# A fused adaLN transformer block on one core: two issuing queues for the second group's stacked rows, and the decay table loaded and exponentiated earlier

## The chip, the cores and the metric

The kernel runs on one core of a Trainium2 chip. That core has a matrix engine (TensorE, PE in the profile), VectorE (DVE), ScalarE (ACT), GpSimd (POOL) and a queue engine that only issues transfers (SyncE, SP). ScalarE can issue transfers too, between its own instructions. The engines run side by side and wait for each other through semaphores written out by hand. The metric is the device time of one execution in microseconds (us); shorter is better.

## The reference

```python
x = L0_attn_x                                       # (8, 256, 128)
mod = (_silu(L0_c) @ L0_wmod).reshape(8, 6, 1, -1)
sa, ca, ga, sb, cb, gb = (mod[:, k] for k in range(6))
ga = (2 * (ga >= 0) - 1) * jnp.maximum(jnp.abs(ga), 0.25)      # gb likewise
h = _layernorm(x) * (1 + ca) + sa
x = x + ga * attention(h)                           # 16 heads of 8
h = _layernorm(x) * (1 + cb) + sb
x = x + gb * moe(h)                                 # 16 experts, top 2, plus a shared one
# attention:
scores = einsum('bqhd,bkhd->bhqk', q, k) * 8 ** -0.5
decay = jnp.exp(-alpha * |i - j|)
attn = softmax(scores * decay);  out = (attn @ v) @ Wo.T + bo
```

All values are float32. Eight sequences of 256 tokens are computed.

## The kernel before, in words

The 2048 tokens are cut into four chunks of 512 (two sequences each). In each chunk the attention runs in eight "quads" q = 0 to 7: a quad is four heads of one sequence, and two quads (one per sequence) make a group g of heads. For one quad PE computes four score matrices (`scores`, L914), DVE multiplies them by the decay table and takes the row maximum (`head`, L681), POOL turns them into maximum minus score (`negdiff`, L279), PE transposes them (`turn`, L930, in two halves of two heads), ACT takes the exponential (`exps`, L384) and PE multiplies by the values (`values`, L942). PE's program interleaves them: scores of quad q, first half of the turn of quad q-1, values of quad q-2, second half of the turn of quad q-1. After the four chunks comes the mixture of experts (from L1148 on PE).

The scores need float32 accuracy from faster matmuls. So q and k are split in a high and a low part (`qk_hi_of` on ACT, L362, and `qk_lo_of` on DVE, L601), and for each head the four combinations high/high, high/low, low/high and low/low are stacked as rows of one 32-row operand. The stacking is done by transfers: `stack_slot` (L148) copies 32 partitions of q and k, 128 KB, into every fourth partition of `qk_st`, and a group needs its four slots before its scores can start. Slot 0 needs the two high parts, slot 2 the low part of q, slots 1 and 3 the low part of k. Group 0 of chunk 0 is made in another way (`first`, `first_hi`, `first_lo`), without transfers. All other groups are stacked by SP (`stack`, L181), in the order group 1, 2, 3 of chunk 0 and then the later chunks. For group 1 SP issues slot 0, 2, 1, 3, one after the other.

The prologue, before that: SP loads the first half of chunk 0 of x, the conditioning, its weights, an identity, the other half of x, the first weights, then the table of lags (`load(decay...)`, L176), and more. ACT issues three small loads (L503 to L505), computes the SiLU of the conditioning and one dummy exponential that brings in the table of functions. DVE computes the layer norm of the first two tiles (`stats_first`, `xn_first`), then copies the modulation vectors, then waits for lags and alpha and negates alpha (L789 to L790). PE fills its waits with matmuls on zeros (`warm`, L1100), transposes the normalised tiles (`lnt_first`), and ACT makes the first affine copy (`h_first(0)`, L523), then the exponential of the lags (L526), then `first_hi(0)`. In chunk 0 POOL computes the layer norm constants of chunk 1 (`ln1(1)`) before the maximum differences of head 8, ACT then normalises chunk 1's tiles (`xn_of(1)`, L357), and PE transposes them (`lnt(1)`) right after the scores of quad 3 and ahead of the turn of quad 2.

Of the kernel before, what the change touches and what calls it, by code (L numbers as in the profile page):

```python
# [10 lines left out]
ALU = mybir.AluOpType  # L11
ACT = mybir.ActivationFunctionType
AX_X = mybir.AxisListType.X

P = 128
# [12 lines left out]
SLOTS = 4  # L28
# [22 lines left out]
def build(nc, x, x_t, c_t, w_first, v_first, w_attn, vecs, alpha, w_r, w_gu, w_d, w_mod, lag, ident, out):  # L51
# [3 lines left out]
    with ExitStack() as ctx:  # L55
        def sb(name, shape, dt=F32):
            return ctx.enter_context(nc.sbuf_tensor(name, shape, dt))
# [6 lines left out]
        decay = sb("decay", [P, BPC, SEQ])  # L64
        alpha_sb, nalpha = sb("alpha_sb", [P, 1]), sb("nalpha", [P, 1])
# [82 lines left out]
        def stack_slot(eng, g, slot):  # L148
            bq, bk = SLOT_BLOCKS[slot]
            eng.dma_start(qk_st[slot:P:SLOTS, :, g, :].bitcast(F32),  # L150
                          qk[32 * g:32 * g + 32, bq:bk + 1:bk - bq, :].bitcast(F32)).then_inc(s_st[g], 16)
# [13 lines left out]
        @block.sync  # L165
        def _(sp):
            def load(ap, dram, done):
                sp.dma_start(ap, dram).then_inc(s[done], 16)  # L168

            load(x_all[:, 0:BPC, :], x_v[:, 0:BPC, :], "ld_x0")  # L170
            load(ct_sb[:], c_t, "ld_ct")
            load(wmod_sb[:, SA:CA1 + 1, :], w_mod[:, SA:CA1 + 1, :], "ld_mod")
            load(id_f[:], ident, "ld_id")
            load(x_all[:, BPC:TT, :], x_v[:, BPC:TT, :], "ld_x0b")
            load(wf_sb[:], w_first, "ld_first")
            load(decay[:], lag, "ld_decay")  # L176
            load(wmod_sb[:, GA_IN:, :], w_mod[:, GA_IN:, :], "ld_mod_b")
            load(wa_sb[:], w_attn, "ld_attn")
            load(x_all[:, TT:, :], x_v[:, TT:, :], "ld_x")

            def stack(c, g):  # L181
                if c:
                    if g == 0:
                        sp.wait_ge(s["qk_lo_ok"], c * 2 + 2)
                    sp.wait_ge(s["s_done"], (c - 1) * STEPS + 8 * g + 8)
                    for slot in range(SLOTS):
                        stack_slot(sp, g, slot)
                    return
                for slot, (done, count) in ((0, ("qk_hi_ok", 2)), (2, ("qk_lo_ok", 1)),
                                            (1, ("qk_lo_ok", 2)), (3, ("qk_lo_ok", 2))):  # L190
                    if g == 1:
                        sp.wait_ge(s[done], count)
                    stack_slot(sp, g, slot)

            def weights_out(c):
                sp.wait_ge(s["cwt_ok"], c + 1)
                sp.dma_start(cw_dram[c], cw_t[:]).then_inc(s["cw_out"], 16)

            def weights_in(c, u):
                if c:  # L200
                    sp.wait_ge(s["mul_done"], (c - 1) * ROUTED + u + 1)
                for k in range(2):
                    e = 2 * u + k
                    sp.dma_start(cwb[k * FE:k * FE + FE, u, :],
                                 cw_dram[c, e:e + 1, :].to_broadcast([FE, CHUNK])).then_inc(s_cwb[u], 16)

            def out_of(c):
                cols = slice(c * CHUNK, c * CHUNK + CHUNK)
                sp.dma_start(out[:, cols], xt[:, cols]).then_inc(s_out, 16)

            for c in range(NCHUNK):
                for g in range(NG):
                    if c or g:
                        stack(c, g)
                    if c == 0 and g == NG - 1:
                        for ap, dram in ((wr_sb[:], w_r), (wgu_sb[:], w_gu), (wd_sb[:], w_d)):
                            load(ap, dram, "ld_ffn")
                for k in {1: (0,), 2: (1,), NCHUNK - 1: (2, 3)}.get(c, ()):
                    sp.wait_ge(s["wlo_ok"], 2 * k + 2)
                    cols = slice(k * CHUNK, k * CHUNK + CHUNK)  # L220
                    sp.dma_start(xt[:, cols], x_t[:, cols]).then_inc(s_xt[k], 16)
            weights_out(0)
            sp.wait_ge(s["cw_out"], 16)
            for u in range(ROUTED):
                weights_in(0, u)
            weights_out(1)

            for c in range(NCHUNK):
                for u in range(ROUTED):
                    if c + 1 < NCHUNK:  # L230
                        if u == 0:
                            sp.wait_ge(s["cw_out"], 16 * (c + 2))
                        weights_in(c + 1, u)
                    if u == LAG_D + 2 and c:
                        sp.wait_ge(s["y_added"], c)
                        out_of(c - 1)
                if c + 2 < NCHUNK:
                    weights_out(c + 2)
            for b in range(BPC):
                cols = slice((NB - BPC + b) * SEQ, (NB - BPC + b + 1) * SEQ)  # L240
                sp.wait_ge(s["y_added"], NCHUNK + b)
                sp.dma_start(out[:, cols], xt[:, cols]).then_inc(s_out, 16)
            sp.wait_ge(s_out, 16 * (NCHUNK + 1))
# [98 lines left out]
        def _(act_e):  # L342
# [19 lines left out]
            def qk_hi_of(c, i, ps):  # L362
                act_e.wait_ge(s["qk_mm"], c * 2 + i + 1)
                if c and i == 0:
                    act_e.wait_ge(s_st[NG - 1], c * STACK)
                nc.scalar.activation(qk[:, (Q_HI, K_HI)[i], :], ps[:], ACT.Identity,
                                     bias=vec_sb[:, (B_Q, B_K)[i]:(B_Q, B_K)[i] + 1],
                                     scale=1.0).then_inc(s["qk_hi_ok"], 1)
# [108 lines left out]
            def chunk(i):  # L477
                prev, nxt = i > 0, i < NCHUNK - 1
                for q in range(QUADS):
# [20 lines left out]
                    if (i, q) in SPLITS:  # L500
                        split(SPLITS.index((i, q)))

            act_e.dma_start(vf_sb[:], v_first).then_inc(s["ld_vf"], 16)  # L503
            act_e.dma_start(alpha_sb[:], alpha.to_broadcast([P, 1])).then_inc(s["ld_decay"], 16)
            act_e.dma_start(vec_sb[:], vecs).then_inc(s["ld_attn"], 16)  # L505
            act_e.wait_ge(s["ld_ct"], 16)
            nc.scalar.activation(silu_c[:], ct_sb[:], ACT.Silu).then_inc(s["silu_ok"], 1)
            act_e.wait_ge(s["pool_init"], 1)
            nc.scalar.activation(spare[:], nhalf[:], ACT.Exp)

            def h_first(b, ready, done):
                act_e.wait_ge(s[ready], 1)
# [8 lines left out]

            act_e.wait_ge(s["modt_ok"], 2)
            h_first(0, "lnt_a", "h_a")  # L523
            act_e.wait_ge(s["ld_decay"], 32)
            act_e.wait_ge(s["nalpha_ok"], 1)
            nc.scalar.activation(decay[:], decay[:], ACT.Exp, scale=nalpha[:, 0:1]).then_inc(s["decay_raw"], 1)  # L526
            act_e.wait_ge(s["ld_vf"], 16)
            first_hi(0)
            h_first(1, "lnt_done", "h_ok")
            first_hi(1)  # L530
            qk_hi_of(0, 0, ps_t[0])
            qk_hi_of(0, 1, ps_t[1])
            for i in range(NCHUNK):
                chunk(i)
            exps(NCHUNK - 1, QUADS - 1, 0)
# [53 lines left out]
        def _(dve):  # L589
# [171 lines left out]
            def stats_first(tiles_, loaded, st_done, done):  # L761
                dve.wait_ge(s[loaded], 16)
                for t in tiles_:
                    last = nc.vector.bn_stats(stats[:, t, :], x_all[:, t, :])
                last.then_inc(s[st_done], 1)
                dve.wait_ge(s[st_done], 1)
                for t in tiles_:
                    last = nc.vector.bn_aggr(mv[:, t, :], stats[:, t, :])
                last.then_inc(s[done], 1)

            def xn_first(tiles_, ready, done):
                dve.wait_ge(s[ready], 1)
                for t in tiles_:
                    last = nc.vector.tensor_scalar(xn[:, t, :], x_all[:, t, :], mv[:, t, 0:1], rstd[:, t:t + 1],
                                                   ALU.subtract, ALU.mult)
                last.then_inc(s[done], 1)
# [5 lines left out]
                                               ALU.subtract).then_inc(s["first_ok"], 1)  # L782

            stats_first(range(0, BPC), "ld_x0", "stats_a", "mv_a")
            xn_first(range(0, BPC), "rstd_a", "xn_a")
            dve.wait_ge(s["modt_mm"], 1)
            nc.vector.tensor_copy(mod_t[:, SA, :], ps_s[0][:, 0:NB]).then_inc(s["modt_ok"], 1)
            nc.vector.tensor_scalar(mod_t[:, CA1, :], ps_s[0][:, NB:2 * NB], 1.0, None, ALU.add).then_inc(s["modt_ok"], 1)
            dve.wait_ge(s["ld_decay"], 32)  # L789
            nc.vector.tensor_scalar(nalpha[:], alpha_sb[:], -1.0, None, ALU.mult).then_inc(s["nalpha_ok"], 1)  # L790
            stats_first(range(BPC, TT), "ld_x0b", "stats_ok", "mv_ok")
            first_lo(0, 0)
            first_lo(0, 1)
# [92 lines left out]
        def _(pe):  # L886
# [213 lines left out]
            def warm(n, ps=ps_o):  # L1100
                for k in range(n):
                    mm(ps[:, 0:P], attn_t[:, 0:P], attn_t[:, 0:P])
# [15 lines left out]
            def first(b, k):  # L1118
                mm(ps_first[2 * b + k][:, 0:SEQ], wf_sb[:, k, :], h_t[:, seq_cols(b)]).then_inc(s["first_mm"], 1)

            warm(2)
            pe.wait_ge(s["ld_id"], 16)
            lnt_first(0, "xn_a", "lnt_a")
            warm(3)
# [141 lines left out]
```

## Time and profile before

| | us |
|---|---|
| median of 3 runs (lowest, highest) | 242.24 (242.0, 243.11) |
| the profiled execution, its own time | 243.98 |
| the span of that profile | 242.2 |
| PE / DVE / ACT / POOL busy | 230.0 / 192.3 / 161.8 / 188.8 |

Times in the rows below count from the start of the span. The span is 1.8 us shorter than that execution's own time, and the execution was 1.7 us longer than the median run. "Idle before" is the time for which an engine stood still ahead of an instruction, with what ended it. An engine name with a q (SPq, ACTq) is its sequencer, and a DMA_DIRECT2D on it is the issue of one transfer.

### The profile page before, as it was taken

How to read it: one execution, taken by the hardware profiler on the slowest of the kernel's cores; microseconds unless marked ns; L12 is line 12 of the kernel's file. 1: busy time of each engine (PE TensorE's matmuls, PEld its weight loads, DVE VectorE, ACT ScalarE, POOL GpSimd, SP SyncE). 2: the span in 40 equal slices, each digit the busy share in tenths (PEclk: the TensorE clock that was granted, in tenths of full speed). 3: DMA queues.
4: the chain of work that ended last, by engine and by line, in shares of the span. 5: the costliest groups of instructions: out<-in, count | busy, mean ns of one | idle time of the engine just before them, and what ended most of it. 6: DMA issues, size and time to landing. Idle time of an engine off the chain costs nothing.

```text
span 242.2 us, 5876 instructions
## 1 busy us (share of the span) xinstructions
PE 230.0 (95%) x1866; PEld 171.5 (71%) x1866; DVE 192.3 (79%) x800; ACT 161.8 (67%) x318; POOL 188.8 (78%) x343
## 2 busy tenths in 40 slices
PE   7996999998999999999999999999999999999994
PEld 7764666766657767657767766677888888788882
DVE  3697868898799799899989997469656786985763
ACT  4455668667866798866896578576647758565550
POOL 5579778899999999997999999718477554676661
PEclk9998899999999999999999999999999999999998
DMA  5718902760004730004755500014223340036311
GB/s 131 228 25 193 305 38 54 186 155 3 0 4 102 201 91 4 0 3 117 187 144 186 164 0 5 3 47 131 102 78 131 126 136 1 0 91 198 110 43 43
DMA packets 15342, 22.81 MB, mean 94 GB/s; under 512 B 3088, under 2 KB 5776, under 8 KB 15184
## 3 DMA queue, kind: packets, MB, share of 16 engines
q1 hardware_dynamic: 14880, 22.44, 32.7%
q8 instruction: 15, 0.25, 0.4%
q14 instruction: 15, 0.12, 0.2%
q10 hardware_dynamic: 432, 0.01, 0.1%
HBM read 13.39 MB, written 1.18 MB: 60 GB/s over the span
## 4 chain that ended last, share of the span: by engine, by line
PE 60%; POOL 14%; DVE 12%; ACT 5%; DMA 3%; issue 2%; SPq 2%; DVEq 0%; ACTq 0%
PE bank L888 60%; POOL sc L285 12%; DVE sc L686 4%; DVE sc L852 2%; DMA decay<-in_lag 1%; DMA qk_st<-qk 1%; SPq L168 1%; ACT L553 1%; SPq L150 1%; DVE h_lo L634 1%; DVE pr L846 1%; DVE qk L604 1%; POOL rstd L258 1%; DVE qk_st L780 1%; ACT act_hi L544 1%
## 5 line engine op out<-in xcount | busy, mean ns | idle before, releaser
L285 POOL TENSOR_SCALAR sc<-sc,mx 128x256 f32<-128x256 f32 x256 | 122.2, 496 | 7.8 <-DVE mx L686 7.7
L686 DVE CUSTOM_DVE_ANT_0 sc<-bank,decay 128x256 f32<-128x256 f32 x256 | 91.4, 420 | 14.6 <-PE bank L888 14.3
L389 ACT ACTIVATE pr<-bank 128x512 f32<-128x512 f32 x128 | 69.6, 597 | 25.3 <-PE bank L888 25.1
L888 PE MATMUL bank<-id_f,sc 128*128 128x128 f32 x512 | 69.5, 278 | 2.2 <-ACT pr L389 1.1
L332 POOL TENSOR_TENSOR act_lo<-sc,act_hi 128x512 fp32r<-128x512 f32 x35 | 45.3, 1296 | 33.2 <-ACT act_hi L544 33.2
L888 PEld LDWEIGHTS bank<-id_f,sc 128*128 128x128 f32 x512 | 56.8, 142 | 14.9 <-issue 6.7
L888 PE MATMUL bank<-pr,v_one 128*32 128x256 f32 x512 | 35.1, 393 | 0.0
L846 DVE TENSOR_TENSOR pr<-bank,cwb 128x512 f32<-128x512 f32 x32 | 22.0, 688 | 14.5 <-PE bank L888 14.2
L553 ACT ACTIVATE bank<-bank 128x512 f32<-128x512 f32 x32 | 18.6, 582 | 18.7 <-PE bank L888 18.4
L852 DVE TENSOR_TENSOR sc<-pr,bank 128x512 f32<-128x512 f32 x36 | 24.7, 687 | 5.8 <-ACT bank L553 2.7
L888 PE MATMUL bank<-h_hi,wgu_hi 128*128 128x512 f32 x72 | 28.5, 395 | 0.0
L888 PE MATMUL bank<-h_lo,wgu_hi 128*128 128x512 f32 x72 | 28.1, 391 | 0.0
L888 PE MATMUL bank<-h_hi,wgu_lo 128*128 128x512 f32 x72 | 28.0, 389 | 0.0
L544 ACT ACTIVATE act_hi<-sc 128x512 fp32r<-128x512 f32 x36 | 22.5, 624 | 3.7 <-DVE sc L852 3.4
L888 PEld LDWEIGHTS bank<-pr,v_one 128*32 128x32 f32 x512 | 13.5, 110 | 13.3 <-issue 5.0
L686 DVE DVE_READ_ACCUMULATOR2_ANT mx<- 128x1 f32 x256 | 21.2, 83 | 0.0
L888 PE MATMUL bank<-qk_st 32*128 32x256 f32 x256 | 16.3, 327 | 4.4 <-DMA qk_st<-qk 2.0
L888 PEld LDWEIGHTS bank<-qk_st 32*128 32x128 f32 x256 | 9.8, 183 | 10.0 <-issue 6.1
L888 PEld LDWEIGHTS bank<-h_hi,wgu_hi 128*128 128x128 f32 x72 | 13.5, 188 | 3.1 <-issue 0.4
L888 PEld LDWEIGHTS bank<-h_lo,wgu_hi 128*128 128x128 f32 x72 | 13.5, 188 | 2.9
L888 PEld LDWEIGHTS bank<-h_hi,wgu_lo 128*128 128x128 f32 x72 | 13.5, 188 | 2.7
L888 PE MATMUL bank<-act_hi,wd_hi 128*128 128x512 f32 x36 | 15.0, 416 | 0.0
(105 smaller groups left out, 281.6 us busy)
## 6 DMA issues: line engine op xcount, KB each, us to landing
cwb<-cw_dram SPq DMA_DIRECT2D x64, 128.0 KB, 3.0
qk_st<-qk SPq DMA_DIRECT2D x60, 128.0 KB, 2.7
wgu_sb<-in_w_gu SPq DMA_DIRECT2D x1, 1152.0 KB, 5.7
wgu_sb<-in_x_t SPq DMA_DIRECT2D x4, 256.0 KB, 3.9
x_all<-in_x SPq DMA_DIRECT2D x1, 768.0 KB, 6.5
out_dram<-wgu_sb SPq DMA_DIRECT2D x3, 256.0 KB, 3.1
wd_sb<-in_w_d SPq DMA_DIRECT2D x1, 576.0 KB, 6.6
x_all<-in_x SPq DMA_DIRECT2D x2, 128.0 KB, 2.6
```

The costliest lines, as they stand in the source:

```text
L150: eng.dma_start(qk_st[slot:P:SLOTS, :, g, :].bitcast(F32), qk[32 * g:32 * g + 32, bq:bk + 1:bk - bq, :].bitcast(F32)).then_inc(s_st[g], 16)
L168: sp.dma_start(ap, dram).then_inc(s[done], 16)
L258: nc.gpsimd.tensor_tensor(rstd_[:], var_[:], nhalf[:], ALU.pow).then_inc(s[done], 1)
L285: last = nc.gpsimd.tensor_scalar(sc[:, n % RING, t, :], sc[:, n % RING, t, :], -1.0, mx[:, n % RING, t:t + 1], ALU.mult, ALU.add)
L332: nc.gpsimd.tensor_tensor(act_lo[:, (i * NU + u) % FR, :], act[:, (i * NU + u) % FR, :], act_hi[:, (i * NU + u) % FR, :].bitcast(F32), ALU ...
L389: nc.scalar.activation(pr[:, n % RING, :, :].rearrange("p a b -> p (a b)"), turn_bank(i, n)[:], ACT.Exp, scale=-1.0).then_inc(s["exp_done" ...
L544: nc.scalar.activation(act_hi[:, (i * NU + u) % FR, :], act[:, (i * NU + u) % FR, :], ACT.Copy).then_inc(s["ahi_ok"], 1)
L553: nc.scalar.activation(gate[:], gate[:], ACT.Silu).then_inc(s["silu_done"], 1)
L686: last = nc.vector.tensor_tensor_reduce(sc[:, n % RING, t, :], ps_s[n % SB][:, t * SEQ:t * SEQ + SEQ], decay[:, t, :], float(HD) ** -0.5, ...
L846: nc.vector.tensor_tensor(gate_u[:, n % 2, :], up[:], cwb[:, u, :], ALU.mult).then_inc(s["mul_done"], 1)
L852: nc.vector.tensor_tensor(act[:, r, :], gate_u[:, n % 2, :], (gate if u < ROUTED else up)[:], ALU.mult).then_inc(s["act_ok"], 1)
L888: return nc.tensor.matmul(o, l, r, start=start, stop=stop, skip_group_check=not check, is_transpose=transpose or None)
```

## The change

The second group's (g = 1) four stacking transfers in chunk 0 are shared between two queues: SP issues slots 2 and 1, ACT issues slots 0 and 3. Alpha and the lags are issued by ACT as its first two loads, instead of SP's seventh and ACT's second. The exponential of the lags stands ahead of `h_first(0)` on ACT, and the negation of alpha with its wait for both loads stands ahead of `xn_first` on DVE. PE's filler ahead of the first transposes is one matmul instead of two.

```diff
@@ sync
             load(wf_sb[:], w_first, "ld_first")
-            load(decay[:], lag, "ld_decay")
             load(wmod_sb[:, GA_IN:, :], w_mod[:, GA_IN:, :], "ld_mod_b")
...
-                for slot, (done, count) in ((0, ("qk_hi_ok", 2)), (2, ("qk_lo_ok", 1)),
-                                            (1, ("qk_lo_ok", 2)), (3, ("qk_lo_ok", 2))):
-                    if g == 1:
-                        sp.wait_ge(s[done], count)
+                if g == 1:
+                    sp.wait_ge(s["qk_hi_ok"], 2)
+                    sp.wait_ge(s["qk_lo_ok"], 1)
+                    stack_slot(sp, g, 2)
+                    sp.wait_ge(s["qk_lo_ok"], 2)
+                    stack_slot(sp, g, 1)
+                    return
+                for slot in range(SLOTS):
                     stack_slot(sp, g, slot)
@@ scalar
+            act_e.dma_start(alpha_sb[:], alpha.to_broadcast([P, 1])).then_inc(s["ld_decay"], 16)
+            act_e.dma_start(decay[:], lag).then_inc(s["ld_decay"], 16)
             act_e.dma_start(vf_sb[:], v_first).then_inc(s["ld_vf"], 16)
-            act_e.dma_start(alpha_sb[:], alpha.to_broadcast([P, 1])).then_inc(s["ld_decay"], 16)
             act_e.dma_start(vec_sb[:], vecs).then_inc(s["ld_attn"], 16)
...
             nc.scalar.activation(spare[:], nhalf[:], ACT.Exp)
+            act_e.wait_ge(s["ld_decay"], 32)
+            act_e.wait_ge(s["nalpha_ok"], 1)
+            nc.scalar.activation(decay[:], decay[:], ACT.Exp, scale=nalpha[:, 0:1]).then_inc(s["decay_raw"], 1)
...
             h_first(0, "lnt_a", "h_a")
-            act_e.wait_ge(s["ld_decay"], 32)
-            act_e.wait_ge(s["nalpha_ok"], 1)
-            nc.scalar.activation(decay[:], decay[:], ACT.Exp, scale=nalpha[:, 0:1]).then_inc(s["decay_raw"], 1)
             act_e.wait_ge(s["ld_vf"], 16)
...
             qk_hi_of(0, 1, ps_t[1])
+            act_e.wait_ge(s["qk_hi_ok"], 2)
+            stack_slot(act_e, 1, 0)
+            act_e.wait_ge(s["qk_lo_ok"], 2)
+            stack_slot(act_e, 1, 3)
@@ vector
             stats_first(range(0, BPC), "ld_x0", "stats_a", "mv_a")
+            dve.wait_ge(s["ld_decay"], 32)
+            nc.vector.tensor_scalar(nalpha[:], alpha_sb[:], -1.0, None, ALU.mult).then_inc(s["nalpha_ok"], 1)
             xn_first(range(0, BPC), "rstd_a", "xn_a")
...
-            dve.wait_ge(s["ld_decay"], 32)
-            nc.vector.tensor_scalar(nalpha[:], alpha_sb[:], -1.0, None, ALU.mult).then_inc(s["nalpha_ok"], 1)
@@ tensor
-            warm(2)
+            warm(1)
```

## Rows read from the trace of the kernel before

**Rows 1.** Page, the costliest group: count, busy us, mean ns, idle before, releaser.
```profile
L285 POOL TENSOR_SCALAR sc<-sc,mx 128x256 f32<-128x256 f32 x256 | 122.2, 496 | 7.8 <-DVE mx L686 7.7
```
**Rows 2.** Chain of waits: start us, us, what; first stretch to 40 us.
```profile
3.67 3.51 DMA decay<-in_lag
...
14.23 1.41 DVE qk L604 x2
...
15.67 1.80 SPq L150
...
17.51 0.61 SPq L150
...
18.17 3.01 DMA qk_st<-qk
```
**Rows 3.** Timeline of PE: start us, us, operation, idle before and its releaser.
```profile
5.50 0.69 PE L888 MATMUL bank<-attn_t 128*128 128x128 f32 x4
...
18.07 1.12 PE L888 MATMUL bank<-id_f,sc 128*128 128x128 f32 x8 [0.34 <-POOL sc L285]
21.22 0.51 PE L888 MATMUL bank<-qk_st 32*128 32x256 f32 x8 [2.03 <-DMA qk_st<-qk]
21.66 1.37 PE L888 MATMUL bank<-id_f,sc 128*128 128x128 f32 x8
22.95 1.94 PE L888 MATMUL bank<-pr,v_one 128*32 128x256 f32 x16
...
26.27 0.51 PE L888 MATMUL bank<-qk_st 32*128 32x256 f32 x8
26.71 0.66 PE L888 MATMUL bank<-id_f,xn 128*128 128x128 f32 x4
27.20 1.04 PE L888 MATMUL bank<-id_f,sc 128*128 128x128 f32 x8
28.17 1.07 PE L888 MATMUL bank<-pr,v_one 128*32 128x256 f32 x16
```
**Rows 4.** Stretches: us, busy of PE, PEld, DVE, ACT, POOL, clock, DMA share, GB/s.
```profile
20.00:22.00 2.00, 0.78 (x11) 0.65 (x12) 0.55 (x5) 0.00 (x0) 1.83 (x5) 1.00 0.85 205
22.50:25.50 3.00, 3.00 (x22) 1.40 (x21) 2.93 (x17) 2.58 (x6) 2.98 (x8) 0.50 0.85 189
```
**Rows 5.** Timeline of POOL and of ACT around the second group.
```profile
22.52 0.20 POOL L263 TENSOR_TENSOR nmr<-nmean,rstd 128x4 f32<-128x4 f32 x1
...
27.69 3.70 POOL L285 TENSOR_SCALAR sc<-sc,mx 128x256 f32<-128x256 f32 x8 [1.27 <-DVE mx L686]
32.51 0.94 POOL L285 TENSOR_SCALAR sc<-sc,mx 128x256 f32<-128x256 f32 x2 [1.12 <-DVE mx L686]
...
17.33 1.09 ACT L389 ACTIVATE pr<-bank 128x512 f32<-128x512 f32 x2 [2.49 <-PE bank L888]
23.56 1.64 ACT L357 ACTIVATE xn<-x_all,nmr,rstd 128x128 f32<-128x128 f32 x4
```
**Rows 6.** The DMA queues while SP issues slot 2 (15.7 to 17.4 us).
```profile
q8 instruction: 1, 0.02, 4.6%
...
qk_st<-qk SPq DMA_DIRECT2D x1, 128.0 KB, 3.9
```
**Rows 7.** Timeline of ACT and DVE in the prologue.
```profile
4.17 0.21 ACT L507 ACTIVATE silu_c<-ct_sb 128x8 f32<-128x8 f32 x1 [0.76 <-DMA ct_sb<-in_c_t]
5.70 0.21 ACT L509 ACTIVATE spare<-nhalf 128x4 f32<-128x4 f32 x1
6.52 0.56 ACT L344 ACTIVATE h_t<-bank,mod_t 128x256 f32<-128x256 f32 x1 [0.61 <-PE bank L888]
7.46 0.72 ACT L526 ACTIVATE decay<-decay,nalpha 128x512 f32<-128x512 f32 x1 [0.38 <-DVE nalpha L790]
8.09 1.00 ACT L519 ACTIVATE act_hi<-bank,vf_sb 128x256 fp32r<-128x256 f32 x2
4.97 0.60 DVE L774 TENSOR_SCALAR xn<-x_all,mv,rstd 128x128 f32<-128x128 f32 x2 [1.11 <-POOL rstd L311]
```
## The prediction

> **What bounds the kernel now.** I read three views in this order. The page first: PE is busy for 230.0 of 242.2 us, and the costliest group on another engine is POOL's maximum differences, 122.2 us of work with 7.8 us of idle time before it, 7.7 of that spent waiting for DVE's maxima [rows 1]. So PE sets the pace of the attention and POOL runs close behind it. What the change can give back must therefore be a place where PE stands still, and it must pass POOL as well. The chain of waits next: up to 21 us it leaves PE twice for a transfer, once for the lags, 3.51 us from their issue, and once for the four slots of group 1 [rows 2]. There the reader sees DVE finish the low parts at 15.64, the issue of slot 2 take 1.80 us where that of slot 1 takes 0.61, and the last slot land 3.01 us after its issue began, at 21.18 [rows 2]. PE's timeline last: PE ends the second half-turn of quad 0 at 18.07 + 1.12 = 19.19, stands still for 2.03 us, and starts the scores of quad 2 at 21.22 [rows 3]. After that stop its clock is granted at 0.50 from 22.5 to 25.5, which is the lower of its two levels, 1.2 GHz, where it had 1.00 between 20 and 22 [rows 4]. The values of quad 0 then take 1.94 us where those of quad 1 take 1.07 [rows 3].
>
> **The change part by part.**
>
> *The second queue.* The last landing is four issues behind the low parts today. SP issues slot 0 ahead of 15.67, slot 2 (1.80 us) from there, slot 1 at 17.51 and slot 3 at 18.17 [rows 2]. With two queues slots 0 and 2 go out side by side before 15.64, and slots 1 and 3 side by side from about 15.67. The long issue coincides with one packet of 16 KB on an instruction queue [rows 6], and I expect the second pair to meet it as slot 2 does now: both issues end near 17.47. Slot 2, issued in the same way, landed 3.9 us after 15.67 [rows 6], at 19.57. A pair moves twice the bytes, and a slot's bytes take at most the spacing of two slots, 18.17 - 17.51 = 0.66 [rows 2]: 20.2 if the pair shares one rate, 19.6 if it doesn't. I take 20.1. Bounds: 21.2 when nothing is won, and 19.19, where PE is free, when the issues don't stall. Gain at PE's stop: 21.22 - 20.1 = 1.1 us, between 0 and 2.03.
>
> The Trainium skill ("Runtime: NRT & Kernel Launch", section "Instruction fetch mechanics") says that engines stream their program in blocks of 16 KiB and that crossing into a block is mostly hidden. The row disagrees: an issue of 1.80 us beside such a packet, against 0.61. By the page the pair would be issued by 16.3 and PE would not stop at all; by the row it stops for about 0.9 us. The sum below is the same either way.
>
> What ACT pays: two issues and a wait for DVE's low part at 15.64, between its last high part and its first exponential of quad 0. Queued behind them are the exponentials that PE's turns and values wait for. They start at 17.33 after 2.49 us of idle time [rows 5]; both issues end inside it, or, if the second stalls until 17.47, 0.14 us after it, which PE's remaining stop covers. Without that cover it would cost up to 1.2 us, the excess of 1.80 over 0.61. I take nothing. SP's next groups move up by two issues; nobody waits for them.
>
> *The clock.* From the start of the half-turn at 21.66 to the scores of quad 3 at 26.27 PE needs 4.61 us for half-turn, values, half-turn [rows 3]. At the full clock a half-turn takes 28.17 - 27.20 = 0.97 and values about 1.0, so 2.94. The low clock costs 4.61 - 2.94 = 1.67 us. With a stop of 0.9 us instead of 2.03 I expect that it doesn't fall; the bounds are 0 and 1.67.
>
> *What is late next.* PE would reach the scores of quad 3 at 20.1 + 0.44 + 2.94 = 23.5 instead of 26.27. Behind them stand the transposes of chunk 1's normalised tiles (26.71 now). They need ACT's four activations, 1.64 us [rows 5], which need POOL's constants. POOL ends these at 22.72 [rows 5], in a series of its own that began with DVE's maxima of quad 1 and that the group's landing doesn't touch. So ACT ends at 22.7 + 1.64 = 24.35 and PE's transposes at 24.8; the first half-turn of quad 2 follows there instead of at 27.20. That is 2.4 us, where stop and clock together would give 2.8.
>
> *Whether 2.4 reaches the end.* POOL's differences of quad 2 still start at 22.7. What POOL gains is its idle time behind them: 1.27 before 27.69 and 1.12 before 32.51 [rows 5], 2.39 together, and more after it out of the 7.7 [rows 1]. By 33 us POOL is ahead by as much as PE. Everything later waits on engines alone, so it moves up.
>
> *The prologue.* Now the lags land at 7.18 [rows 2] and their exponential holds `first_hi(0)` until 8.09 [rows 7]. In the new order that exponential follows the dummy one (5.70 + 0.21), and its successor can start 8.09 - 7.46 = 0.63 later [rows 7]: `h_first(0)` at 5.95 + 0.63 = 6.58 against 6.52, so the removed filler (half of 0.69 us [rows 3]) brings nothing, since ACT is late instead of PE. `first_hi(0)` comes 8.09 - 6.52 = 1.57 us behind `h_first(0)` now, part of it because the exponential stands between (7.46 + 0.63 is just 8.09). Without it PE's first weights alone decide; my estimate is 1.4 to 1.5 behind 6.58, thus 8.0: a gain of 0.1, at worst none. Against it: 256 KB of lags now enter the queues ahead of the conditioning, which releases the SiLU at 4.17 after 0.76 us of waiting [rows 7] and has the table load, the dummy and now the lags' exponential behind it without slack. The lags took 3.51 us from their issue in the thick of the other loads; issued second by ACT, near 1.2, they land near 4.7 at that rate, and the conditioning could slip to that: a loss of 0.5, with DVE's two small copies and the first transposes beside it perhaps 0.7. I take a loss of 0.2, range -0.1 to +0.7. `first_lo`, the high and low parts of group 1 and POOL's constants all hang on this chain, so it counts in full. The wait put ahead of DVE's `xn_first` (4.97 now) costs nothing while the lags land before about 5.2.
>
> **The sum.** Against the profiled execution (243.98, that is 242.2 of span and 1.8 around): -2.4 + 0.2 = -2.2, so 241.8. The median of the runs shown is 242.24, 1.74 below that execution, and this is nearly the price of the low clock, 1.67. I can't tell from one profile whether the timed runs are shorter because they lack that fall or because they lack the profiler. If the median run had none of it, PE would reach the first half-turn of quad 2 at 25.5 (27.20 - 1.67) already, the gain would be 25.5 - 24.8 = 0.7 and with the prologue 0.5 to 0.6: 241.6. If it had all of it: 240.0. The highest run shown, 243.11, lies 0.9 to 1.1 above the others, which looks like a fall that hits some executions wholly and some in part. I take about half: 0.75 + 0.8 - 0.2 = 1.4, thus 240.8.
>
> **The rivals.**
>
> 1. *The engines, not the issues, pace the slots.* Four slots land 0.66 apart, and the DMA engines are busy at 0.85 with 205 GB/s then [rows 4]. If that is their rate for such copies, two queues only mix them, and SP's slots of group 2, issued right behind slot 1, take a share from slot 3: it lands near 21.0. For it: the share. Against it: of the time from 15.64 to 21.18, 1.19 us is the excess of one issue [rows 2], which is no work of the engines. Time: 0.2 gained, the clock falls as before, prologue 0.2 lost: 242.2. The Trainium skill ("DMA: Bandwidth & Descriptors", section "Issuing engines are not separate DMA queues") speaks for this one: transfers of different issuers interleave on the same 16 engines and a second issuer saves issue time only.
>
> 2. *The median never had the low clock,* and only the wait counts: 241.6. For it: the 1.74 us between profile and median. Against it: the run at 243.11.
>
> 3. *The median had it in full,* 240.0.
>
> 4. *DVE's wait for the lags becomes the bound,* and the kernel is slower. DVE holds the normalised tiles until the lags have landed. If they land at D, PE's transposes and `h_first(0)` come at D + 1.3, so from D = 5.2 each us counts fully against 6.52 + 0.06. If the traffic and not the time of issue set their landing at 7.18, this costs 8.5 - 6.58 = 1.9 us, while the gain is 0.7 to 2.4: 243.4 with the small gain. The break-even is D = 6.0 to 7.7, by the gain that it has to eat. For it: the queues are dense from 3 us on. Against it: issued 2.5 us earlier they meet only x's first half and the small loads.
>
> **How the numbers follow.** Forecast 240.8 (its own range 240.2 to 241.4) 0.43; rival 3 0.15; rival 2 0.22; rival 1, or a loss in the prologue that eats the gain, 0.13; rival 4 0.07. The range of 8 in 10 reaches from 239.6, the full clock with no loss in the prologue and a bit beyond, to 242.2. About 0.5%, 1.2 us, is what a measurement of this kernel tells from no change, so faster means below 241.0: rival 3 and two thirds of the forecast and some of the rest with a small loss, 0.52; same 0.41; slower 0.07.
>
> **What would show it.** Right: PE's idle time ahead of the scores of quad 2 is near 0.9 or less (2.03 now); the clock stays at 1.00 between 22 and 26 us; the first half-turn of quad 2 starts near 25 and waits behind the transposes, released by ACT; POOL has no idle time before quads 3 and 4; ACT's exponentials of quad 0 start near 17.4. The prologue's step: the SiLU starts between 4.2 and 4.8, and `first_hi(0)` between 8.0 and 8.5. Wrong: the last slot lands after 20.8, the clock falls in spite of the shorter stop, DVE's `xn_first` is released by the lags' load, or the gain is there at 30 us and gone at 60, which would mean that POOL and not PE carries it.

## The result and the profile after

| | before | after |
|---|---|---|
| median of 4 runs each, us | 242.68 (242.0 to 243.28) | 245.93 (244.34 to 246.62) |
| the profiled execution, its own time / span, us | 243.98 / 242.2 | 246.06 / 244.2 |

The ratio is 1.0127, 95% interval 1.0097 to 1.0156: the change makes the kernel about 3 us slower. I had forecast 240.8, faster. A second set of the same changed kernel gave 245.48 (ratio 1.0111, 1.0083 to 1.0139). Three disturbed executions in all the sets below, of 260, 370 and 545 us, are left out of every figure.

The prologue comes first. These are ACT and DVE of the changed kernel, and they answer to [rows 7]:

```profile
5.33 0.21 ACT L511 ACTIVATE silu_c<-ct_sb 128x8 f32<-128x8 f32 x1 [1.40 <-DMA ct_sb<-in_c_t]
6.85 0.20 ACT L513 ACTIVATE spare<-nhalf 128x4 f32<-128x4 f32 x1
6.96 0.71 ACT L516 ACTIVATE decay<-decay,nalpha 128x512 f32<-128x512 f32 x1
7.96 0.56 ACT L347 ACTIVATE h_t<-bank,mod_t 128x256 f32<-128x256 f32 x1 [0.28 <-PE bank L896]
10.09 0.56 ACT L526 ACTIVATE act_hi<-bank,vf_sb 128x256 fp32r<-128x256 f32 x1 [1.57 <-PE bank L896]
...
4.32 0.48 DVE L772 BATCH_NORM_STATS2 stats<-x_all 128x6 f32<-128x128 f32 x2 [2.94 <-DMA x_all<-in_x]
5.16 0.15 DVE L794 TENSOR_SCALAR nalpha<-alpha_sb 128x1 f32<-128x1 f32 x1
6.20 0.60 DVE L782 TENSOR_SCALAR xn<-x_all,mv,rstd 128x128 f32<-128x128 f32 x2 [0.89 <-POOL rstd L314]
```

The SiLU starts at 5.33 instead of 4.17 and the normalised tiles at 6.20 instead of 4.97: x and the conditioning have both landed 1.2 us later. (In four later profiles with the same early loads x is as late, 4.34 to 4.38, but the SiLU starts at 4.52 to 4.57.) The lags have landed by 5.16, so DVE's new wait holds nothing; the releaser is POOL. `first_hi(0)` starts at 10.09 instead of 8.09, after 1.57 us of waiting for PE. PE's timeline says why, and goes on to the second group; it answers to [rows 3]:

```profile
5.78 1.02 PE L896 MATMUL bank<-silu_c,wmod_sb 128*128 128x8 f32 x4 [0.56 <-DMA wmod_sb<-in_w_mod]
...
8.93 1.91 PE L896 MATMUL bank<-h_t,wf_sb 128*128 128x256 f32 x4
...
12.02 0.51 PE L896 MATMUL bank<-qk_st 32*128 32x256 f32 x8 [0.19 <-DVE qk_st L788]
...
13.63 1.13 PE L896 MATMUL bank<-h_t,wf_sb 128*128 128x256 f32 x4
...
20.43 1.11 PE L896 MATMUL bank<-id_f,sc 128*128 128x128 f32 x8 [0.34 <-POOL sc L288]
23.29 0.51 PE L896 MATMUL bank<-qk_st 32*128 32x256 f32 x8 [1.74 <-DMA qk_st<-qk]
23.73 1.22 PE L896 MATMUL bank<-id_f,sc 128*128 128x128 f32 x8
24.87 1.94 PE L896 MATMUL bank<-pr,v_one 128*32 128x256 f32 x16
...
29.27 1.04 PE L896 MATMUL bank<-id_f,sc 128*128 128x128 f32 x8
```

The same four matmuls of the first weights take 1.91 us at 8.93 and 1.13 at 13.63: PE is at its low level in the first case. The windows print 1.00 for that stretch because the trace has no clock record before the first rise; the durations decide there. The rise comes at 10.9 (5.3 in the profile of before). PE had stood still for 0.56 us ahead of 5.78 while still at the low level. The scores of quad 0 start at 12.02 against 9.66, 2.36 us late.

The stop before quad 2 is 1.74 us, not 0.9, and the clock falls after it: a window of the changed kernel (columns as in [rows 4]):

```profile
25.00:27.50 2.50, 2.50 (x20) 1.23 (x21) 2.43 (x13) 2.11 (x6) 2.50 (x7) 0.50 0.74 166
```

The chain of waits has the last slot, against [rows 2]:

```profile
16.59 0.68 DVE qk L612
...
17.34 0.77 SPq L150
18.11 0.04 issue
18.16 5.09 DMA qk_st<-qk
```

No issue is long this time (0.77 where [rows 2] have 1.80), the pair is out by 18.9, and yet the last slot lands 5.09 us after 18.16, at 23.25. From the end of the low parts (17.98) that is 5.3 us, hardly better than the 5.5 of before with its long issue. Both profiles keep their difference from here on: 29.27 - 27.20 = 2.07 at the half-turn of quad 2, and 246.06 - 243.98 = 2.08 at the end.

### The profile page after: what moved, and what is told of

Read it like the earlier page. It is cut to its first block, busy times and chain, and to the rows that moved or that the text cites. A ratio compares the mean times of both kernels' runs of the same rounds, so it can differ in the third digit from the quotient of the medians.

```text
span 244.2 us, 5873 instructions
## 1 busy us (share of the span) xinstructions
PE 232.2 (95%) x1864; PEld 173.3 (71%) x1864; DVE 193.2 (79%) x800; ACT 161.9 (66%) x318; POOL 188.6 (77%) x343
## 4 chain that ended last, share of the span: by engine, by line
PE 62%; POOL 14%; DVE 12%; ACT 5%; DMA 4%; issue 2%; SPq 1%; DVEq 0%
PE bank L896 62%; POOL sc L288 12%; DVE sc L694 4%; DMA qk_st<-qk 2%; DVE sc L860 2%; DMA wmod_sb<-in_w_mod 2%; ACT L561 1%; DVE h_lo L642 1%; DVE pr L854 1%; POOL rstd L261 1%; ACT act_hi L552 1%; ACT bank L561 1%; ACT pr L392 1%; DVE cw L686 1%; DVE qk_st L788 1%
## 5 line engine op out<-in xcount | busy, mean ns | idle before, releaser
L392 ACT ACTIVATE pr<-bank 128x512 f32<-128x512 f32 x128 | 69.6, 597 | 24.8 <-PE bank L896 24.8
```

What stands on the lines that cost most here:

```text
L392: nc.scalar.activation(pr[:, n % RING, :, :].rearrange("p a b -> p (a b)"), turn_bank(i, n)[:], ACT.Exp, scale=-1.0).then_inc(s["exp_done" ...
```

## The experiments

"Last slot" is the time from the end of DVE's second low part to the landing of the last slot of group 1. Times are medians; ratios are to the kernel before, run beside it on the same chip. "Theory A" and "Theory B" are those of the expectation just above. An execution with a fallen clock has a mean granted clock of 0.993 or less over its span, the others 0.997 or more. In the edits, words stand for code lines that were moved.

**Loads alone.**

```diff
-            load(decay[:], lag, "ld_decay")                  # SP
+            alpha, lags, vf, vec as ACT's loads, in this order
```

> The kernel before with only the loads moved: alpha and the lags are ACT's first two loads, nothing else is changed. Theory A (the lags' 256 KB, issued early, delay x, the conditioning and its weights by about 1.2 us, and PE's stop for them delays the rise of its clock): slower by 1.5 to 2.5 us, the SiLU near 5.3 instead of 4.17, PE's matmuls at half speed until 8 us or later. Theory B (the loss comes from the new order on ACT and DVE and from the missing filler): within 0.5 us of the kernel before.

244.32 us, ratio 1.0044 (1.0012 to 1.0077). ACT's SiLU waits until 5.3 and DVE's statistics until 4.29, as in the changed kernel:

```profile
4.29 0.49 DVE L764 BATCH_NORM_STATS2 stats<-x_all 128x6 f32<-128x128 f32 x2 [2.91 <-DMA x_all<-in_x]
```

The landing part of theory A holds; the clock part doesn't in this execution: it rose at 4.5, ahead of PE's 0.80 us stop, and stayed. The price, 1.1 us, is below the expected 1.5.

**Stacking alone.**

```diff
+            SP issues slots 2, 1; ACT issues slots 0, 3
```

> The kernel before with only the stacking of group 1 shared between SP and ACT. Theory A (two queues bring the last slot only 0.3 us nearer to the low parts, as in the changed kernel's profile, because the copies share the same DMA engines): 0 to 0.4 us faster, PE's stop before the scores of quad 2 about 1.7, the clock falls after it as before. Theory B (my forecast: the second queue was worth 1.1 us and was hidden in the changed kernel by the later prologue): 0.7 to 2.4 us faster.

243.05, ratio 1.0026 (1.0002 to 1.0050). Slower, outside both theories. The last slot lands after 5.2 us:

```profile
16.42 5.01 DMA qk_st<-qk
```

The clock has fallen in 4 of 12 executions, at 244.2 to 244.9. The others have a median of 242.7, where those of the kernel before beside them have 242.5: what the two queues cost here is mostly the more frequent fall.

**The changed kernel with stacking on SP alone.**

```diff
-            two queues
+            slots 0, 2, 1, 3 by SP, as before
```

> The changed kernel with the stacking back on SP alone: loads, order of the exponential and the negation, and the filler as changed. Theory A (all the loss is the prologue's, the stacking gives 0.3 back): 3.3 to 3.7 us slower than the kernel before, that is 0 to 0.4 more than the changed kernel. Theory B (the ACT queue's part in the stacking costs something): equal to or faster than the changed kernel, under 3 us slower than the kernel before.

243.92, ratio 1.0048 (1.0028 to 1.0068). Theory A is wrong: the prologue is not all of the loss, and the stacking gives nothing back. Last slot 4.65 us, stop 1.13, scores of quad 0 at 11.36, clock rising at 9.4. The clock has fallen in 4 of 12 executions (3 of 29 of the kernel before beside it), though the stacking is the old one; the other 8 have a median of 243.4, 0.9 above those of the kernel before.

**Ten fillers instead of eight in the changed kernel.**

```diff
-            warm(8)
+            warm(10)
```

> The changed kernel with ten instead of eight filler matmuls on PE before the modulation, so that PE has no idle time while it waits for the late weights. Theory A (about half of the prologue's loss is PE at its low clock, which rises later because PE stood still for 0.56 us): 0.7 to 1.3 us faster than the changed kernel, the first transposes and first weights at full speed. Theory B (the loss is the later loads alone): equal to the changed kernel or up to 0.4 us slower.

245.12, ratio 1.0105 (1.0071 to 1.0138). Its interval overlaps the changed kernel's, so the runs don't tell the theories apart. The clock rose at 4.5 in its profile and the scores of quad 0 started at 10.54. With the loads alone and the same early rise they start at 10.50. So in the changed kernel the late rise costs about 12.02 - 10.54 = 1.5 us where it happens. This profile loses them again at the slots: a stop of 2.04 us, and then the low level from 22 to 28 us, about twice as long as in the changed kernel (columns as in [rows 4]).

```profile
22.11 0.80 PE L896 MATMUL bank<-qk_st 32*128 32x256 f32 x8 [2.04 <-DMA qk_st<-qk]
...
22.00:28.00 6.00, 5.89 (x39) 4.07 (x40) 4.72 (x21) 2.97 (x7) 5.11 (x11) 0.50 0.80 222
...
29.40 1.04 PE L896 MATMUL bank<-id_f,sc 128*128 128x128 f32 x8
```

The half-turn of quad 2 starts at 29.40, against 29.27 in the changed kernel.

**A filled stop in the kernel before.**

```diff
+                    if i == 0 and q == 2:
+                        pe.wait_ge(s["gate_a"], 1)
+                        warm(8)
                     scores(i, q)
```

> The kernel before with eight filler matmuls on PE ahead of the scores of quad 2, in the stop. Theory A (the clock falls only in the few executions in which the stop is long: 3 of 29 runs of the kernel before, at 244.1 to 244.7 against 242.5 for the others; the usual stop is 1.2 us, shorter than the 1.8 us of filler): no execution with a fallen clock, but the filler ends 0.5 us after the slots, median equal or up to 0.4 us slower, spread smaller. Theory B (my forecast: half of the clock's price is in the median): 0.5 to 1.2 us faster.

242.84, ratio 1.0014 (0.9992 to 1.0035), no fallen clock in 12. Theory A. This takes away what I had put half of my gain on.

**Two queues with group 2 held back.**

```diff
+                if g == 2:
+                    sp.wait_ge(s_st[1], STACK)
```

> The stacking on two queues alone (kernel before otherwise), and SP waits with group 2's slots until group 1 has landed. Theory A (the engines set the pace, and group 2's slots from SP take their turns between slot 3's packets from ACT): the last slot lands 4.4 to 4.8 us after the low parts instead of 5.2 to 5.3, the stop is 1.2 or less, the clock falls more rarely than in 4 of 12 runs, time equal to the kernel before. Theory B (two queues issuing at once slow each other whatever follows): last landing still 5.1 or more.

242.70, ratio 1.0005 (0.9984 to 1.0026). The last slot still needs 5.06 us, the stop is 1.53, and the clock has fallen in 3 of 12. Theory B: group 2's slots are not what delays slot 3.

**Alpha first, lags with SP.**

```diff
-            vf, alpha, vec by ACT
+            alpha, vf, vec by ACT
```

> The kernel before with alpha as ACT's first load instead of its second; the lags stay with SP. Theory A (the lags' 256 KB are what delays the first loads): x lands at 3.1 and the SiLU starts at 4.2 as before, same time. Theory B (alpha's 128 packets of 4 bytes, issued together with x, are what delays it): x lands near 4.3, SiLU near 5.3, 1 to 1.5 us slower.

242.80, ratio 1.0011 (0.9988 to 1.0034). x is late by 0.9 us, the SiLU (4.35) by 0.2:

```profile
3.98 0.49 DVE L764 BATCH_NORM_STATS2 stats<-x_all 128x6 f32<-128x128 f32 x2 [2.60 <-DMA x_all<-in_x]
...
7.74 0.15 DVE L790 TENSOR_SCALAR nalpha<-alpha_sb 128x1 f32<-128x1 f32 x1 [1.14 <-DMA decay<-in_lag]
```

Both theories are half right. Alpha's packets delay x. The lags, when they are early too, delay the conditioning's weights: PE waits for them until 5.47 to 5.78 in six of the seven profiles with both loads early, and not at all here (5.01). The conditioning itself they delay in some profiles (5.33, 5.32, 5.31) and hardly in others (4.52 to 4.57). In this kernel the later x is covered, because the lags (7.74) still hold `first_hi(0)`.

**Lags as ACT's fourth load.**

```diff
-            load(decay[:], lag, "ld_decay")
+            act_e.dma_start(decay[:], lag)      # behind vf, alpha, vec
```

> The kernel before with the lags issued by ACT as its fourth load (from 2.1 us) instead of by SP as its seventh (from 3.7). Theory A (what hurts is that the lags are in the queues together with x and the conditioning): x lands at 3.1 and the SiLU starts at 4.2 to 4.6, lags land by 6, time from 0.3 faster to 0.4 slower. Theory B (any big load on the second queue delays SP's first ones): SiLU at 5 or later, 1 us slower.

242.47, ratio 0.9999 (0.9977 to 1.0021). x lands as before, the SiLU starts at 4.12, the lags are there by 5.68, the scores of quad 0 start at 9.52. Theory A. This profile, with a clock that never falls, also shows what stands behind the stop:

```profile
19.83 0.51 PE L888 MATMUL bank<-qk_st 32*128 32x256 f32 x8 [0.79 <-DMA qk_st<-qk]
...
24.38 0.63 PE L888 MATMUL bank<-id_f,xn 128*128 128x128 f32 x4 [0.55 <-ACT xn L356]
24.86 1.11 PE L888 MATMUL bank<-id_f,sc 128*128 128x128 f32 x8
...
22.58 1.65 ACT L356 ACTIVATE xn<-x_all,nmr,rstd 128x128 f32<-128x128 f32 x4 [0.53 <-POOL nmr L262]
```

PE waits 0.55 us for ACT's normalised tiles of chunk 1, and ACT waited for POOL's constants.

**The changed kernel again.**

> The changed kernel itself again, beside the others of this set, since only four executions of it are known and all four had a fallen clock. Theory A (the losses add up and the fall of the clock is only more frequent than in either part alone): some executions without the fall near 244.0, as with the kernel of ten fillers, most with it near 245.5 to 246.5, median 1.0 to 1.3% slower. Theory B (the parts just add, 0.5% of the prologue and 0.3% of the stacking): 0.7 to 0.8% slower.

245.48, ratio 1.0111 (1.0083 to 1.0139). With the first four, 9 of 10 executions have a fallen clock. Theory A.

**A half-turn in the stop.**

```diff
+                    if i == 0 and q == 2:
+                        turn(0, 1, 0)          # ahead of scores(0, 2), not behind
```

> The kernel before with PE doing the first half-turn of quad 1 ahead of the scores of quad 2 instead of behind them, so that a piece of real work of 1.0 us stands in the stop. Theory A (the stop is 1.15 us in the usual execution and only the part beyond ACT's normalised tiles is lost): stop 0.1 to 0.2, no fallen clock, 0.3 to 0.9 us faster. Theory B (DVE's maxima of quad 2 wait for the scores, and POOL passes nothing on): no change within 0.3 us.

242.64, ratio 0.9995 (0.9979 to 1.0012), no fallen clock in 12, and a narrow spread (242.04 to 243.26). Theory B. What replaces the stop is a wait of the same size one quad later:

```profile
19.93 1.12 PE L888 MATMUL bank<-id_f,sc 128*128 128x128 f32 x8 [0.40 <-ACT pr L389]
20.98 0.51 PE L888 MATMUL bank<-qk_st 32*128 32x256 f32 x8
21.41 1.07 PE L888 MATMUL bank<-pr,v_one 128*32 128x256 f32 x16
22.41 1.09 PE L888 MATMUL bank<-id_f,sc 128*128 128x128 f32 x8
24.41 0.51 PE L888 MATMUL bank<-qk_st 32*128 32x256 f32 x8 [0.90 <-DVE mx L686]
```

The half-turn itself starts only at 19.93, released by ACT, and so pushes the scores to 20.98.

**The same with the lags as ACT's fourth load.**

> The same with the lags issued by ACT as its fourth load. Theory A (both gains are real and separate): 0.2 to 0.5 us faster than with the half-turn first alone, 0.5 to 1.2 us faster than the kernel before. Theory B (the start is not on the path once the lags are early): equal to the half-turn first alone.

242.45, ratio 1.0009 (0.9981 to 1.0037). Theory B at best: nothing measurable.

**The new order with the lags as ACT's fourth load.**

```diff
+            DVE: ld_decay wait and nalpha ahead of xn_first
+            ACT: exponential of the lags ahead of h_first(0)
-            warm(2)
+            warm(1)
```

> The changed kernel's order (negation of alpha ahead of the tiles on DVE, exponential of the lags ahead of the first affine copy, one filler fewer) with stacking on SP alone and the lags as ACT's fourth load, behind alpha. Theory A (the order costs little: DVE waits for the lags until about 5.7 instead of starting the tiles at 4.97, and the first affine copy follows the exponential): 0.3 to 1.0 us slower than the same loads in the old order, 242.8 to 243.5. Theory B (the order is free or a gain): 242.0 to 242.5.

243.19, ratio 1.0024 (0.9998 to 1.0051), 0.7 above the same loads in the old order: theory A by the medians, though the two intervals overlap. Here DVE's new wait is the one that I had named for rival 4:

```profile
5.91 0.15 DVE L786 TENSOR_SCALAR nalpha<-alpha_sb 128x1 f32<-128x1 f32 x1 [2.02 <-DMA decay<-in_lag]
5.98 0.59 DVE L774 TENSOR_SCALAR xn<-x_all,mv,rstd 128x128 f32<-128x128 f32 x2
```

Its clock also rises late, at 10.0, so the start of its scores of quad 0 (11.41) is not the order's doing alone.

**The changed kernel with the half-turn in the stop.**

> The changed kernel with PE's first half-turn of quad 1 ahead of the scores of quad 2, so that the stop holds work and is shorter. Theory A (of the changed kernel's 1.1 to 1.3%, 1.3 to 1.8 us are the fall of the clock behind the long stop, which hits nearly every execution): no or rare fallen clock, 243.6 to 244.3, that is 1.2 to 1.9 us faster than the changed kernel and 0.4 to 0.7% slower than the kernel before. Theory B (the loss sits in the prologue alone and the fall is a mark, not a cause): 245 or more.

244.26, ratio 1.0062 (1.0037 to 1.0087), a fallen clock in 1 of 6. Theory A: 1.2 us under the changed kernel's second set. The stop ahead of the scores of quad 2 is 0.25. It is also 1.1 us under the changed kernel with the second filler back (245.37, the last run below), which ran beside it.

**All four slots on ACT's queue.**

```diff
+            ACT: slots 0, 2, 1, 3;  SP: sp.wait_ge(s_st[1], STACK) before group 2
```

> The kernel before with all four slots of group 1 issued by ACT, in the old order, and SP waiting with group 2 until they have landed. Theory A (it is two queues running side by side that makes the copies slower): the last slot lands 4.3 to 4.7 us after the low parts, as with SP alone, and packets take about 133 ns instead of 165 to 175. Theory B (ACT's queue is the slow one): 5.0 or more.

242.85, ratio 1.0000 (0.9975 to 1.0026). The last slot lands after 4.34 us. Issues of ACT and the scores of quad 2 in this kernel:

```profile
15.42 2.71 ACTq L150 DMA_DIRECT2D qk_st<-qk  x4
...
20.55 0.51 PE L895 MATMUL bank<-qk_st 32*128 32x256 f32 x8 [0.53 <-DMA qk_st<-qk]
```

Four issues in a row take 2.71 us and are out at 18.13, 2.0 us behind the low parts; with two queues and group 2 held back both pairs are out 0.9 us behind them, and the last slot lands later. Window of the four copies with one queue, and with two (columns as in [rows 4]):

```profile
15.50:20.00 4.50, 3.87 (x32) 3.38 (x32) 4.15 (x24) 1.83 (x4) 3.23 (x8) 1.00 0.50 118
```

```profile
15.80:20.90 5.10, 3.24 (x27) 2.71 (x26) 4.31 (x29) 2.60 (x5) 3.83 (x9) 1.00 0.55 104
```

Per GB/s the engines are busy for a quarter longer: 0.55 / 104 against 0.50 / 118. The mean duration of a 2 KB packet of these copies in the traces is 165 ns (ACT's) and 176 ns (SP's) side by side, 137 ns alone. The last packet ends 4.0 us behind the low parts with two queues and 3.9 with one; from there to the landing it takes another 1.1 and 0.5 us. Theory A.

**The second filler back.**

```diff
-            warm(1)
+            warm(2)
```

> The changed kernel with the second filler matmul put back ahead of the first transposes. Theory A (ACT and not PE is late there, so the filler costs nothing, and its removal opened no stop of PE either): equal to the changed kernel within 0.4 us, clock still rising late. Theory B (the missing filler is what keeps the clock down until 11 us): 0.7 to 1.2 us faster than the changed kernel.

245.37, ratio 1.0121 (1.0083 to 1.0159). Theory A as to the time. Its profile has the clock rising at 4.6, so the late rise isn't a fixed trait of the changed kernel.

## Why the prediction was wrong

Two steps failed and one term was too small. The step that a second queue brings the last slot 1.1 us earlier had the wrong sign. The step that the median run would gain 0.7 us from the wait alone, and half of the clock's price on top, took both from one unusual execution. And the prologue's loss, taken as 0.2 us, is 1.2.

**What bounds the kernel, read from one execution.** I took the stop of 2.03 us and the fall of the clock for the kernel's habit. Over four sets the kernel before ran 109 times: the clock had fallen in 10, at a median of 244.27, and had not in 99, at 242.59. The profiled 243.98 was one with the fall. Its stop was long because of the long issue. In seven other profiles with stacking on SP alone the issue of slot 2 took 0.62 to 0.64 us, in one 1.40, again beside a 16 KB packet on the instruction queue. With short issues and one queue the last slot needs 4.31 to 4.72 us, and the stops of PE in the old order of its work are 0.8 to 1.2 us. So the wait that the change was to shorten is about 1.1 us, not 2.03. The step "I take about half" of the clock's price should have been a tenth, and nothing for the median. The time of the profiled execution, above all runs shown then, was the warning, and I named it without following it.

**What is late next: right, and it leaves the usual wait without a price.** I had ACT's normalised tiles hold the first half-turn of quad 2 at 24.8, which is 15.1 us behind the scores of quad 0 (9.66). Ten profiles have no fall there. In eight of them this distance is 15.33 to 15.36 us, whether PE stopped for the slots for 1.20, 1.13, 0.79 or 0.53 us or did a half-turn there; in the other two it is 15.66. What is taken from the stop comes back as the wait for the tiles: 1.13 and 0.20, 0.79 and 0.55 us. In the profiles with a fall the distance is 17.1 to 17.5 us (17.54 in the kernel before), and 18.9 in two where the low level lasted about twice as long. So the step "PE would reach the first half-turn of quad 2 at 25.5 (27.20 - 1.67)" subtracted the low clock and kept the stop of 2.03. By these profiles an execution without the fall reaches it at 9.66 + 15.34 = 25.0, where the tiles hold it anyway, and the 0.7 us of gain that rival 2 and the sum were left with were never there. With the half-turn first, DVE's maxima of quad 2 come up at the same place (PE waits 0.90 us for them) and the distance is 15.34 again. No profile of the kernel before itself without a fall exists; the distances are those of its variants.

**The second queue: wrong in sign.** Forecast: slots 1.1 us earlier. Measured: 5.06 to 5.56 us in the seven profiles with two queues against 4.31 to 4.72 with one and no long issue. The same four copies land 0.7 us later side by side (5.06 against 4.34). Rival 1 had the engines as the bound and group 2 as the intruder. The first half points the right way: with the issues out 1.0 us earlier the last packet still ends 4.0 us behind the low parts, against 3.9. The second half is wrong, holding back group 2 doesn't help. The Trainium skill's sentence ("DMA: Bandwidth & Descriptors", "Issuing engines are not separate DMA queues") says that transfers of several issuers interleave on the same 16 engines and that a second issuer saves only the time of issuing. The trace agrees on the issues, 1.0 us of them was saved; beyond what the page says, the slots landed 0.7 us later, 0.1 of it in the packets and 0.6 between the last packet and the landing. Why packets take longer with two queues, and the landing after them too, stays open.

**The clock: price right, direction of its frequency wrong.** Forecast 1.67 us per fall; measured 244.27 - 242.59 = 1.68 in the kernel before, which includes any longer stop of those executions. In other kernels the same difference is 0.9 (prologue alone) to 1.9 us (two queues alone). But the stop grew instead of shrinking. Falls by kernel: 10 of 109 before, 7 of 24 with two queues in the old prologue (stops of 1.66 and 1.53 in the profiles), 9 of 10 with the whole change (1.74 and 1.85), none of 24 with the half-turn in the stop of the kernel before or its lags-last form, 1 of 6 in the changed kernel. The last one shows cause and share: filling the stop takes 1.2 of the 2.9 us away, where the same filling of the kernel before brings nothing. The length of the stop alone doesn't order the counts: with one queue and stops of 0.8 to 1.2 us in the profiles they are 4 of 12 (changed prologue), 1 of 10, 1 of 10, 0 of 12 and 1 of 12. The mean clock doesn't say where in an execution the fall was, and the stops of those that were not profiled aren't known. There was a second effect. In four of the seven profiles with the new order in the prologue PE stood still for 0.2 to 0.6 us, for the late weights or for DVE's tiles, while its clock was still low, and the rise came at 9.4 to 11.1; in the other three it had come at 4.5 to 5.3, before or just as PE stopped. I had no step for that. Why it rises early in one execution and not in the next isn't settled.

**The prologue: right place, wrong size.** I took a loss of 0.2 with 0.7 as the end of the range. The whole prologue costs 0.48% (1.2 us) with stacking on SP, and 0.62% (1.5 us) with two queues and the stop filled. The mis-sized terms: x, which I held to be safe in its place, slipped by 1.23 and with it DVE's tiles, in every profile with both loads early, mostly because of alpha's packets beside it (0.9). The conditioning slipped to the 4.5 to 4.7 that I had as the bad case in four of those profiles and to 5.3 in three, the changed kernel's among them. The late rise of the clock added up to 1.5 where it happened. The gain of the new order, 0.1, isn't there: with loads that don't disturb, the order costs 0.7 by medians (243.19 against 242.47; the intervals of the ratios overlap), and the trace puts it at DVE's wait for the lags. That was rival 4's mechanism, but at D = 5.9 and not by itself the cause in the changed kernel, where the lags land at 5.16.

**The removed filler** costs and gives nothing that can be measured, as forecast. **ACT's two issues** were covered: its first exponential had 2.49 us of idle time ahead in both profiles.

Of the parts, none helped. The sum: with the stop filled the change costs 1.5 us, of which the prologue alone is 1.2, and the clock, which falls nearly always when the late prologue and the long stop come together, adds 1.2: 2.7 of the 2.7 to 3.1 us that the two ratios give. (The 1.2 of the prologue alone includes its own 4 falls in 12.) No variant beats the kernel before measurably; the two with the lowest ratios, the half-turn first (0.9995) and the lags as ACT's fourth load (0.9999), are equal to it.

## What to carry to other kernels

Before pricing a wait from one profile, compare that execution's time and clock with the other runs: a wait that is long because of a one-off may not be in the median at all. Measure the distance between two fixed points around the wait in several variants: if it doesn't change with the wait, something else bounds that stretch. Moving a transfer forward moves it ahead of something; list every load that was in the queues at that time and ask which of them has no slack, small broadcast loads included. Splitting short on-chip copies between two issuing queues is worth a test of its own, since what it saves in issue time it can lose before the landing.

## What the hardware showed

- Four 128 KB copies within on-chip memory, on two queues side by side: packets of 165 to 176 ns against 137 ns with one queue, and a last landing 5.06 us behind the low parts against 4.34, of which 1.1 and 0.5 us stand behind the last packet.
- Alpha's load (128 packets of 4 bytes) as the first of ACT's queue delays x's 128 KB on SP's queue by 0.9 us, from 3.10 to 3.98.
- The clock of PE is low after stops of 1.53 to 2.04 us in all seven profiles that have such a stop, and not after those of 0.53 to 1.20 us in six; by their mean clocks the executions of one kernel differ in it. In the kernel before a fall goes with 1.68 us.
- An issue of an on-chip copy takes 0.61 us in a row, and 1.80 and 1.40 us beside a 16 KB packet on the instruction queue, ending 0.38 us after that packet.
